# Writing out VectorE's loop over fourteen image pairs in the expert stage of a convolution and expert kernel

## The reference

```python
x = x + conv_block(layernorm_over_channels(x))   # sign activations, 3x3 then 1x1 convolution
t = tokens(x)                                    # 32 images x 3136 pixels, 64 channels each
h = layernorm(t)
probs = softmax(h @ gate_w + gate_b)             # 8 experts
idx, prb = argmax(probs), max(probs)             # one expert a token
pos = running place of the token in its expert; kept = pos < C
y = relu(h @ w1[idx] + b1[idx]) @ w2[idx] + b2[idx]
t = t + nan_to_num(y * (prb * kept))             # clipped to +-10000
```

## Time and profile before

| what | value |
|---|---|
| median of 3 runs | 1861.85 us (1861.76 to 1863.74) |
| the profiled execution's own time | 1857.47 us |
| its span, first to last instruction | 1855.7 us |
| PE busy, share of the span | 1568.8 us, 85% |
| DVE busy | 1474.4 us, 79% |
| ACT busy | 1233.0 us, 66% |
| POOL busy | 1048.2 us, 56% |
| DVE's loop of seven turns, first to last branch instruction | 1199.6 to 1815.0 us |

### The profile page before, as it was taken

One profiled execution on the slowest core, in us unless ns is written; L12 is line 12 of the kernel. 1 busy time (PEld: TensorE's weight loads), 2 busy tenths in 40 slices (PEclk: granted clock), 3 DMA queues, 4 the chain that ended last, 5 costly groups with the idle time before them and its releaser, 6 DMA issues.

```text
span 1855.7 us, 41100 instructions
## 1 busy us (share of the span) xinstructions
PE 1568.8 (85%) x10341; PEld 847.0 (46%) x10341; DVE 1474.4 (79%) x3641; ACT 1233.0 (66%) x4066; POOL 1048.2 (56%) x1052
## 2 busy tenths in 40 slices
PE   6998898888888988887612999998989898989894
PEld 1343444433443433344401555565656565656562
DVE  3588978888788888888840888887878797979795
ACT  4778877688787778866511777765656565656561
POOL 3115665766566766666773666654545455545452
PEclk9998988989999999997755999999999999999996
DMA  9446976866555965443425877878979888888895
GB/s 237 77 109 142 177 173 131 178 145 166 144 145 112 164 150 142 119 99 96 104 80 151 243 200 196 231 218 254 289 241 306 249 283 266 270 268 273 260 298 200
DMA packets 302238, 351.92 MB, mean 190 GB/s; under 512 B 48452, under 2 KB 252452, under 8 KB 295940
## 3 DMA queue, kind: packets, MB, share of 16 engines
q1 hardware_dynamic: 260644, 264.23, 54.6%
q0 software_dynamic: 41120, 85.81, 15.3%
q10 hardware_dynamic: 320, 0.33, 0.1%
HBM read 179.70 MB, written 180.01 MB: 194 GB/s over the span
## 4 chain that ended last, share of the span: by engine, by line
PE 45%; DVE 21%; issue 17%; ACT 6%; POOL 6%; DMA 3%; DVEq 1%; SPq 1%; POOLq 0%; ACTq 0%
PE bank L826 10%; PE bank L836 9%; PE bank L735 5%; PE bank L817 4%; POOL pairs_by_group L492 4%; PE bank L697 3%; PE bank L794 3%; PE bank L844 3%; PE bank L745 2%; DVE X L1294 2%; PE bank L768 2%; POOL X L486 2%; DMA pairs_by_group<-ROWS,idx 2%; ACT SQR L960 1%; DVE N L1314 1%
## 5 line engine op out<-in xcount | busy, mean ns | idle before, releaser
L492 POOL DMA_INDIRECT pairs_by_group<-ROWS,idx x400 | 433.4, 1084 | 119.5 <-issue 113.1
L524 POOL DMA_INDIRECT results_by_pair<-X,PAIRNO x310 | 303.2, 978 | 270.5 <-PE bank L817 207.5
L980 ACT ACTIVATE X<-bank,X 128x256 f32<-128x256 f32 x693 | 283.8, 471 | 105.6 <-PE bank L826 105.6
L826 PE MATMUL bank<-X 64*128 64x256 f32 x1848 | 269.4, 410 | 48.7 <-DVE X L1294 48.1
L486 POOL TENSOR_TENSOR X<-Z,X 128x448 f32 (+1 forms) x112 | 141.2, 1261 | 265.0 <-DVE Z L1271 247.1
L836 PE MATMUL bank<-X 128*64 128x256 f32 x1848 | 255.9, 399 | 1.2 <-DVE X L1294 1.2
L735 PE MATMUL bank<-S,WB 128*128 128x448 bf16 x1008 | 231.0, 378 | 0.0
L524 POOL DMA_INDIRECT results_by_pair<-S,PAIRNO x152 | 155.4, 1022 | 105.0 <-PE bank L817 77.3
L973 ACT ACTIVATE X<-bank 128x256 f32<-128x256 f32 x231 | 88.6, 383 | 189.3 <-PE bank L817 186.5
L826 PEld LDWEIGHTS bank<-X 64*128 64x128 f32 x1848 | 168.4, 191 | 99.7 <-issue 85.4
L817 PE MATMUL bank<-ident,X 128*64 128x128 f32 x1848 | 154.9, 289 | 58.6 <-DMA X<-weights_by_group 58.0
(11 more groups left out here) (213 smaller groups left out, 3031.3 us busy)
## 6 DMA issues: line engine op xcount, KB each, us to landing
X<-weights_by_group SPq DMA_DIRECT2D x231, 258.5 KB
X<-pairs_by_group SPq DMA_DIRECT2D x231, 134.0 KB
pairs_by_group<-PAD SPq DMA_DIRECT2D x15, 1742.0 KB
X<-in_x_dram SPq DMA_DIRECT2D x16, 1568.0 KB, 8.1
block_output<-X SPq DMA_DIRECT2D x112, 224.0 KB, 2.0
ROWS<-block_output SPq DMA_DIRECT2D x16, 1568.0 KB
Z<-results_by_pair SPq DMA_DIRECT2D x16, 1568.0 KB, 10.9
out_dram<-ROWS SPq DMA_DIRECT2D x16, 1568.0 KB
```

Source lines behind the costliest of these rows:

```text
L492: pool.indirect_dma_start(rows, bass.IndirectOffsetOnAxis(ap=idx[0:m, p.odd, k:k + 1], axis=0), ROWS[0:m, p.odd, k, :], None).then_inc(s_s ...
L524: pool.indirect_dma_start(done, bass.IndirectOffsetOnAxis(ap=PAIRNO[:, u, j:j + 1], axis=0), RES[u][:, j, :], None,).then_inc(s_back[u], 16)
L826: mm(hidden(q), WR[b, ring, q // 2 * P:(q // 2 + 1) * P], XT[b, ring % 2, :], start=True, stop=True).then_inc(s_h, 1)
L980: last = A(HB[:, ring % 2, q, :], hidden(q), ACT.Relu, bias=WR[:, ring, at:at + 1])
```

## The change

VectorE's loop of seven turns is written out: the `Fori` of the chip becomes a `for` of Python, so that the 168 passes stand one after another in DVE's instruction stream. PE, ACT, POOL and SP have the same instructions as before.

```diff
@@ VectorE's part of the expert stage
             super_pass(2, 2, 0)
             super_tiles(dve, 3, ADD_AT, super_pass)
-            with dve.Fori(0, ROUNDS) as i_n:
+            for i_n in range(ROUNDS):
                 for r in range(SIDE):
                     k = ADD_AT + r
                     super_pass(i_n * SIDE + k, k % RING, i_n * (SIDE // RING) + k // RING)
```

## The result

Written out, the kernel takes 1802.01 us (median of 4 runs, 1795.79 to 1807.55) against 1862.8 us before on the same chip (4 runs, 1861.76 to 1870.42): a ratio of 0.966, with a 95% interval of 0.963 to 0.969. The profiled execution took 1805.56 us with a span of 1803.6, so in the two profiles the spans differ by 52.1 us.

The account below looks back on a forecast made before the run. The prediction saw PE (45% of the span) and DVE (21%) as bounds, plus 17% issue time, partly at DVE's six back edges. Savings of 42.7 + 10.8 = 53.5 us took 1861.85 to 1808.4 us, range 1799 to 1820.

Parts of the forecast that it names:

- The back edges: At the six ends between DVE's seven turns, the fetch stall and what follows it go: 42.7 us saved.
- The separate waits: Ahead of L1316, losing the stand-alone wait saves 0.11 us a pass, counted in seven addition passes a half: 10.8 us.
- The bound of 1.42 us: Most a half could gain in its addition passes before PE sets the pace everywhere; 19.9 us for fourteen halves.
- The sum: Whole kernel: 42.7 + 10.8 = 53.5 us saved, from the median 1861.85 to 1808.4 us; both terms held at 0.74.
- the second term: The gain from stand-alone waits going in DVE's passes: 0.77 us a half, 10.8 us for fourteen.
- The signs named in advance: In the profile: no DVE issue wait above half a microsecond, halves at 40.1 to 40.3 us, clock 1.00, L1316 0.11 us closer.
- Only the back edges: Rival: DVE's 0.11 us a pass returns as a hidden wait, so the gain is 42.7 us, 1819.2 us; chance 0.11.
- Transfers: Rival: DMA becomes the bound once turns shorten, ending at 1817 or 1844 us; chance 0.07.
- 77.8 us of DMA work: DMA work estimated in a turn of one half of each kind, giving a share of 0.97 at 80.4 us a turn.
- Not the branch's: Rival: something else at the turn's end holds DVE and stays, so only 10.8 us come, 1851 us; chance 0.03.
- Late fetches: Rival: straight code is fetched too late, each page crossing stalling 7.1 us, so the kernel gets slower; chance 0.05.

Follow-up runs that it names:

- short loop: The looped kernel before, its body cut from 422 to 375 instructions by removing one wait and no longer putting another apart: 1859.52 us against 1851.45 before.
- written out with separate waits: The written-out change, but with the waits in its 168 passes given instructions of their own again: 1823.54 us, ratio to before 0.984.
- second set of runs: The unaltered change and the kernel before, measured again on the chip that ran the shortened loops: 1804.64 us against 1851.45, ratio 0.974.
- spread additions: The change with the seven additions of a half at passes 2, 3, 5, 6, 8, 9, 11 instead of 5 to 11: 1797.66 us, ratio to before 0.970.
- shifted by 170: The looped kernel before with 170 unused semaphore increments run once ahead of the expert stage: 1888.94 us against 1855.35, ratio 1.021.
- shifted by 64: The looped kernel before with 64 unused semaphore increments run once ahead of the expert stage: 1854.54 us against 1855.35, ratio 1.000.
- shifted by 256: The looped kernel before with 256 unused semaphore increments run once ahead of the expert stage: 1855.56 us, ratio to before 0.999.
- short, shifted by 80: The loop cut to 375 instructions, with 80 semaphore increments run once ahead of the expert stage: 1814.52 us, ratio to the kernel before 0.978.

## Why the prediction was right

**The back edges** were forecast at 42.7 us from the halves with and without one. Two pairs of kernels measured them: 42.5 us (short loop, shifted against not) and 41.9 us (written out with separate waits, against before). Reading the price from whole halves and not from DVE's 27.5 us of gaps was the right choice: PE's slower restart, at a clock of 0.93 in the half, goes with the gap, and without the gap the clock is 1.00.

**The separate waits** were forecast at 0.77 us a half, 10.8 us for fourteen. They measured 0.96 us, 12.5 us for thirteen and so 13.4 for fourteen by estimate. This is the term that was mis-sized. The 0.11 us a pass came from a pass that writes X (idle ahead of L1316 falls by 11.7 us in 105 of them, 0.11 each), and there it was right. In the third of the passes that writes to S, the idle time falls by 0.12 us, and L1315 gets shorter by another 0.06. The bound of 1.42 us, at which PE would have taken over, wasn't reached, and the wait for L1294 that shows DVE still deciding is there, 0.7 us at most.

**The sum** for thirteen halves was 42.7 + 13 x 0.77 = 52.7 us, and 54.4 came. The time, 1802.01 us, stands 6.4 us below the 1808.4 forecast, inside the range. Some 2.6 of this is the second term; the rest is not settled, and that the time came so close is in part luck: the medians fell by 60.8 us here and by 46.8 us in the second set of runs (1851.45 to 1804.64), while the thirteen halves gave 54.4 and 54.8. Medians of the kernel before moved between 1851 and 1863 us from one set of runs to the next, and the start of the expert stage, ahead of which nothing was changed, moved by several us between profiles.

**The signs named in advance** came: no "issue" wait in DVE's list, L1316 0.11 to 0.12 us closer, the clock 1.00 in all thirteen halves, which lie within 0.3 us of one another but for two of 40.36 and 40.58 us. They are a little shorter than the 40.1 to 40.3 us given, as the second term is larger.

**The rivals.** *Only the back edges:* the halves would be 40.9 us, as they are with the separate waits put back; they are 40.0. *Transfers:* the DMA engines do run at 0.93 to 0.96 from the second half on, but no DMA is among the waits of DVE or PE, and with spread additions the halves got shorter still. (The prediction's 77.8 us of DMA work is 77.7 from its own rows, which changes nothing. And that busy times stretch when many packets are in flight holds in the kernel before for some sizes only: packets of 536 bytes took 37 ns in the mean where the engines were 0.6 to 0.8 busy and 51 where the times add up to all 16 engines, those of 2068 bytes 123 and 90.) *Not the branch's:* the same loop at another position has no stall. *Late fetches:* 168 passes of straight code have no "issue" wait. The Trainium skill, page "Runtime: NRT & Kernel Launch", section "Instruction fetch mechanics", says that a long kernel is streamed and that crossing a block's border is mostly hidden; the trace agrees, with DMA engines 0.95 busy.

**What was left open**, why this loop is dearer than the other two, is a matter of position. In the stream of DVE's instructions, separate waits counted too, I laid a border every 128 instructions (a packet is 0.82 MB / 101 = 8.1 KB, so that would be 64 bytes an instruction) so that one falls between the first and the second instruction of the head in the kernel shifted by 170, where the second gap showed it. A block is what lies between two borders. The first two places are good to two instructions, which changes no number of blocks:

| loop | instructions | head's place in its block | blocks from head to branch | after the branch |
|---|---|---|---|---|
| first stage | 351 | 2 | 2 | 0.35 us |
| 12 tiles | 199 | 30 | 1 | 0.20 us |
| seven turns, before | 422 | 85 | 3 | stall |
| shifted by 64 | 422 | 21 | 3 | stall |
| shifted by 170 | 422 | 127 | 4 | two stalls |
| shifted by 256 | 422 | 85 | 3 | stall |
| short | 375 | 50 | 3 | stall |
| short, shifted by 80 | 375 | 2 | 2 | 0.3 us |

It stalls in all cases with three blocks or more between head and branch and in none with two or fewer. The packets bear this out: the loop that doesn't stall fetches about five packets a turn fewer, so it isn't fetched again; and the kernel shifted by 170, whose loop reaches into a fifth block, moved 127 packets of q14 where the kernel before moved 120, one more for each of the six times that it goes back and about one for the 170 instructions. Where the shifts move the loop of 12 tiles so that it too lies over two blocks (by 64, by 170, and in the short kernel by 80), its branch and head stay 0.23 to 0.28 us apart. This is the simplest model that fits. For the two short loops it was a forecast; the other six were at hand when it was made. None was a position chosen to break it. The same section of the Trainium skill speaks of two pages of 256 instructions. With borders 256 apart, the loops at places 85 to 506 and 50 to 424 (stalled) and the one at 130 to 504 (free) would all reach from one page into the next, so this length can't tell them apart; here the runs point to blocks half as long.

**Open:** why L1315 takes 0.34 to 0.54 us in some passes and 0.29 in most, and why, with a separate wait behind it, this happens far more often where it writes to S (32 of 52 passes, against 10 in the change); whether a loop that is shifted, and whose wait between L1315 and L1316 doesn't stand alone, would do as well as the written-out kernel; and where the spread of 8 to 30 us between runs of one kernel comes from (two executions, of 4711 and 7721 us, stand outside it), of which only a part is the start of the expert stage.

## What to carry to other kernels

Where an engine's loop shows idle time with the cause "issue" right behind its branch, look at the sequencer's first instruction at the head and at the packets of the instruction queue: if the head was fetched again, some instructions ahead of the loop can take the stall away as writing it out does (42.5 us here), and can as well cost 4 us or more a turn. Price such a stall from whole periods with and without it, since the engines that wait lose more than the gap (7.1 us a turn here for a gap of 4.6). Then look at waits that stand alone between two operations of a chain: here the one between L1315 and L1316 cost 0.11 to 0.17 us in each pass in which that engine sets the pace, and the others nothing that shows. Written out, its target was a plain number and it sat in its operation. A loop as such doesn't forbid that: in the one here the waits ahead of L1314 and L1315 had register targets and no instruction of their own; for the one ahead of L1316 it wasn't tried.

## What the runs showed that was not expected

A stall at the back edge depends on where the loop lies: 80 instructions that run once, ahead of the stage, made the kernel with the short loop 45 us faster (1859.52 to 1814.52), and 170 made the kernel before 34 us slower (1855.35 to 1888.94). And the second gap, 4.7 us in the kernel shifted by 170, shows that a head on the last place of its block pays for two fetches one after the other.
